# Rearranging three places of a fused two-block network kernel: the zeroing of a scratch array, the rows of maxima in causal attention, and the end of a layer

## The chip, the cores and the metric

The kernel runs on one core of one Trainium2 chip. The metric is the device time of one execution in microseconds (us). Three executions before the change took 4994.17, 4994.56 and 4994.9 us; their median is 4994.56.

## The reference

The input `x` is 4 x 1024 tokens of 128 channels (4096 tokens). Two blocks follow one another, each `x = x + s * silu(g)` with two branches over the same layernorm. Cut to what matters:

```python
xn = layernorm(x)                              # no weights
# block 1
s = attn_in_key_tiles(xn)                      # softmax inside each tile of 128 keys, the 8 tiles averaged by sums
h = xn + causal_attn(rope(conv3(layernorm(xn)) @ attn_w)) @ proj_w   # 16 heads of 8, 1024 tokens
g = h + moe(layernorm(h))                      # top-1 of 4 experts, 512 hidden, silu gate
x = x + s * silu(g)
xn = layernorm(x)
# block 2
s = causal_attn(xn @ w_qkv.T) @ w_proj.T       # 16 heads of 8
g = xn
for i in range(6):                             # 6 layers, 16 heads of 64, windows of 32
    g = g + local_attention(rotary(l2norm(q)), rotary(l2norm(k)), v) @ Wo[i]   # qkv of shift_tokens(g)
    n = layernorm(shift_tokens(g)) * ln_g[i] + ln_b[i]
    a, gate = split(n @ W1[i] + b1[i])         # 341 each
    g = g + (a * gelu(gate)) @ W2[i] + b2[i]
x = x + s * silu(g)
```

The experts work on tokens that are ordered by expert: the kernel scatters them into arrays `sorted_in` in DRAM, whose unused places must be zero.

## The kernel before

The program is one chain of stages, and each stage is one block in which every engine has its own written-out list: TensorE (PE), VectorE (DVE), ScalarE (ACT), GpSimd (POOL) and SyncE (SP, which only issues transfers and waits). A stage opens when the one before it is done on all engines, SP's waits included. Inside a stage the order of each engine is the order of the code, and engines meet by counting semaphores. Activations lie as 128 channels by 4096 tokens; a chunk is 512 tokens (`CH`), a tile 128 (`P`), PSUM is eight banks of 512 f32.

The stages in order: constants, layernorm `ln0`, `tile_attention`, layernorm `ln1`, `causal_convolution`, `causal_inputs`, `causal_attention` `ca0`, `ln2`, `dispatched_experts`, `ln3`, `causal_inputs`, `causal_attention` `ca1`, `shift_tokens`, `layers`, `gate_and_store`.

*The start.* `layernorm` takes a list `fetches`: SP (line 150) issues them all and then waits for all of them (line 152). For `ln0` the list has the remaining constants and tile attention's weights, at most 64 KB each, and last two transfers that fill the two arrays `sorted_in` (19 blocks of 128 x 128 f32, 64 KB, each) from one block of zeros `blank`. In `tile_attention` SP had nothing to do. There POOL first clears the stacks of causal attention (`clear_stacks`, lines 493 to 502) and then scales probabilities (line 465).

*Causal attention.* The work is 16 groups `G` (4 sequences of 1024 tokens by 4 groups of `HG` = 4 heads). A group is 12 units (`UNITS`: 512 queries by 128 keys), and each unit two slots (`two`: a pair of heads); per slot PE makes scores, ACT the exponentials, PE the weighted sums. The scores include minus the row's maximum through two extra rows of the stack `queries`, at `SHIFT_ROW`: the negated maximum in bf16 and its remainder. So while group `G` is worked, the maxima of `G + 1` are made between its slots (`between`, `maximum`, order in `MAXIMA` and `BETWEEN`): PE makes scores once more, in the pair banks 5 and 6 or in the lone bank 7, and DVE reduces them. A bank is taken by `take_pair` or `take_lone` when DVE or ACT has left it. At unit `ROWS_UNIT` = 8 all maxima of the next group are there. DVE negates them into `neg_parts` (`make_rows`), PE turns them into rows (`turn_rows`, line 880): eight products of [128, 8] into the pair banks. ACT copies the rows (`copy_rows`, line 953), SP places them in the next stack by four transfers (`place`, line 753), and the first score of the next group waits for `placed` (line 904). SP also collects the sums of each head and loads the stacks (`load_stack`, line 513). Finished sequences are projected in two halves, `mix`, by a product in the lone bank (line 888) at the units that `FINISH` names; of the 15 changes of group in a stage, 6 have a `mix` at unit 9. `copy_rows` for group `G + 1` stands in ACT's list behind unit 9's first slot.

*Layers.* `steps` lays a tile's operations at fixed distances over 32 tiles (of 128 tokens): `(do, late)` runs `do` for tile `n - late` in step `n`, and `last(...)` only at the last tile. Of a tile, `turn_p` (1653) transposes probabilities, ACT copies them (`out_p`, 1818), `weigh` (1703) makes the heads' outputs, `out_o` (1823) copies them, `project` and `project_rest` (1710) apply `wo`. Behind the last tile begins the second half of the layer, chunk by chunk: `turn` (1730) and `back` (1737) transpose for the layernorm, DVE's `centre` (1974, 1976) and the sums, `square_of` (1846), `norm_invert` (1851, 1853: roots of one of the groups of chunks), `norm_out` (1859), and then the products of the gate (1768) and of the other half (1770), `gelu` (1890), its product on DVE, `down` (1748). `low` (1840) copies what the next shift needs. GELU has its own table in ACT, loaded before the first one (`ACT_TABLE_LOAD`, line 1890).

```python
                    steps((make_next_q, 0), (make_k, 0), (turn_q, 1), (project, 3), (last(lambda: turn(1)), 2), (turn_k, 1),
                          (project_rest, 3), (turn_p, 2), (score, 1), (last(lambda: turn(0)), 1), (make_v, 0), (weigh, 2),
                          (last(lambda: turn(2)), 2))
                    back(0)
```

## Time and profile before

| what | value |
|---|---|
| median of three runs | 4994.56 us |
| profiled execution, its own time | 5013.37 us |
| its span | 5011.6 us |
| PE busy | 4437.7 us (89%) |
| PE weight loads | 2774.2 us (55%) |
| DVE busy | 3689.3 us (74%) |
| ACT busy | 2775.2 us (55%) |
| POOL busy | 2162.7 us (43%) |
| mean granted clock of PE | 0.951 |
| instructions | 169931 |
| DMA queues | 204.72 MB; q1 14.5% of 16 engines, the instruction queues q8 0.8% and q14 0.1% |

The profile is of one execution, which took 5013.37 us, while the three runs without a profile took some 4994.6. Busy times can overlap between engines; PE is the busiest. Of its 40 slices (125 us each) PE is busy by 2 tenths in the first, by 5 to 9 tenths in the next 13, by 9 in all from slice 15 on but the last (8). Weight loads (PEld) run beside products. The granted clock is a share of full speed: 1.00 is 2.4 GHz, 0.50 is 1.2 GHz.

### The profile page before, as it was taken

The page shows a single profiled execution, that of the slowest core. Times are in us where ns is not written, and L with a number is a line of the kernel's source. Part 1 is how long each engine was busy: PE and PEld are TensorE (multiplying, and loading weights), DVE is VectorE, ACT ScalarE, POOL GpSimd, SP SyncE. Part 2 cuts the span into 40 slices and gives each one's busy share as a digit, 9 for nine tenths or more (in the row PEclk, how much of TensorE's full clock was granted, in tenths as well). Part 3 has the DMA queues.
Part 4 walks back from the last instruction along what each step waited for, and adds up shares of the span by engine and source line. Part 5 has one row for each costly group of instructions (what it writes and reads, how often), then busy time and mean ns, then how long its engine had stood idle before and what let it go on. Part 6 is the DMA issues. An engine that isn't in the chain of part 4 may idle for free. (4 is left out here: it accounts for less than half of the span.)

```text
span 5011.6 us, 169931 instructions
## 1 busy us (share of the span) xinstructions
PE 4437.7 (89%) x75610; PEld 2774.2 (55%) x75610; DVE 3689.3 (74%) x4181; ACT 2775.2 (55%) x3767; POOL 2162.7 (43%) x1739
## 2 busy tenths in 40 slices
PE   2876888595898699999999999999999999999998
PEld 1652333363333267765777476756776577646774
DVE  1667887124788488877888688858987799768885
ACT  1644777233677555655665565655655566545664
POOL 1332000313000066645665466636664566546661
PEclk6997999696999899999999999999999999999999
DMA  1002111112011111111111111111111111111110
GB/s 42 1 25 66 39 45 33 60 36 84 25 43 41 54 40 41 41 49 31 41 41 37 44 41 41 41 44 39 41 39 49 36 41 41 38 42 41 39 40 25
DMA packets 108209, 204.72 MB, mean 41 GB/s; under 512 B 28594, under 2 KB 56882, under 8 KB 105650
## 3 DMA queue, kind: packets, MB, share of 16 engines
q1 hardware_dynamic: 105432, 189.65, 14.5%
q8 instruction: 598, 9.80, 0.8%
q0 software_dynamic: 2048, 4.20, 0.3%
q14 instruction: 131, 1.07, 0.1%
HBM read 67.52 MB, written 22.81 MB: 18 GB/s over the span
## 5 line engine op out<-in xcount | busy, mean ns | idle before, releaser
L2044 POOL TENSOR_TENSOR part_of_layer<-part_of_layer,sine_of_layer 128x512 f32<-128x512 f32 x768 | 963.2, 1276 | 620.7 <-DVE sine_of_layer L1920 620.7
L2055 POOL TENSOR_TENSOR part_of_layer<-part_of_layer,inverse_of_layer 128x1024 f32<-128x1024 f32 x384 | 730.1, 1901 | 261.2 <-ACT inverse_of_layer L1803 246.1
L976 ACT ACTIVATE prob_of_ca<-ps 128x1024 f32<-128x1024 f32 (+3 forms) x768 | 591.9, 814 | 245.4 <-PE ps L850 173.0
L1917 DVE TENSOR_TENSOR part_of_layer<-ps,rope 128x1024 f32<-128x1024 f32 x384 | 466.1, 1214 | 33.0 <-ACT square_of_layer L1791 31.4
L1920 DVE TENSOR_TENSOR sine_of_layer<-ps,rope 128x1024 f32<-128x1024 f32 x384 | 464.8, 1210 | 0.0
L1834 ACT ACTIVATE values_of_layer<-ps 128x1024 f32<-128x1024 f32 x192 | 196.5, 1023 | 458.4 <-PE ps L1684 458.4
L868 PE MATMUL ps<-keys_of_ca,queries_of_ca 64*128 64x512 bf16 (+3 forms) x1536 | 325.8, 341 | 133.9 <-DVE top_of_ca L1008 59.7
L1703 PEld LDWEIGHTS ps<-prob_t_of_layer,mixed_of_layer 64*64 64x64 f32 x12288 | 342.4, 135 | 164.1 <-issue 154.5
L1710 PE MATMUL ps<-heads_out_of_layer,wo 128*128 128x128 f32 x3072 | 417.8, 281 | 13.1 <-ACT heads_out_of_layer L1823 12.1
L1956 DVE TENSOR_REDUCE total_of_layer<-prob_of_layer 128x16 f32<-128x1024 f32 x192 | 234.1, 1219 | 237.9 <-ACT prob_of_layer L1827 237.9
L1610 PE MATMUL ps<-qkv,shifted 128*128 128x512 f32 x768 | 383.2, 621 | 24.0 <-POOL values_of_layer L2058 19.9
L1703 PE MATMUL ps<-prob_t_of_layer,mixed_of_layer 64*64 64x32 f32 x12288 | 392.7, 221 | 13.0 <-ACT prob_t_of_layer L1818 6.7
L1703 PE MATMUL ps<-prob_t_of_layer,values_of_layer 64*64 64x32 f32 x12288 | 391.0, 220 | 12.9 <-issue 12.0
L1710 PEld LDWEIGHTS ps<-heads_out_of_layer,wo 128*128 128x128 f32 x3072 | 383.4, 197 | 16.9 <-ACT heads_out_of_layer L1823 16.9
L1684 PE MATMUL ps<-qkv,shifted 128*64 128x512 f32 x1536 | 383.7, 612 | 7.1 <-issue 7.1
L1008 DVE TENSOR_REDUCE top_of_ca<-ps 128x2 f32<-128x1024 f32 (+1 forms) x320 | 357.3, 1117 | 40.2 <-PE ps L868 24.8
L1623 PE MATMUL ps<-qkv,shifted 128*128 128x512 f32 x768 | 362.8, 595 | 12.0 <-DVE sine_of_layer L1920 12.0
L1703 PEld LDWEIGHTS ps<-prob_t_of_layer,values_of_layer 64*64 64x64 f32 x12288 | 345.2, 135 | 18.8 <-issue 17.4
L1813 ACT ACTIVATE keys_of_layer<-ps 128x1024 f32<-128x1024 f32 x192 | 196.8, 1025 | 248.9 <-PE ps L1642 248.9
L919 PE MATMUL ps<-prob_of_ca,values_of_ca 128*32 128x512 f32 (+3 forms) x3072 | 327.2, 498 | 0.7 <-ACT summed_of_ca L962 0.7
L1964 DVE TENSOR_TENSOR prob_of_layer<-prob_of_layer,total_of_layer 128x1024 f32<-128x1024 f32 x192 | 318.4, 1658 | 6.6
L1671 PE MATMUL ps<-keys_of_layer,queries_of_layer 64*32 64x64 f32 x24576 | 298.7, 228 | 4.1 <-issue 3.2
(237 smaller groups left out, 8831.1 us busy)
## 6 DMA issues: line engine op xcount, KB each, us to landing
mixed_of_layer<-values_of_layer SPq DMA_DIRECT2D x636, 128.0 KB
mixed_of_layer<-values_of_layer SPq DMA_DIRECT2D x264, 64.0 KB
queries_of_ca<-q_parts SPq DMA_DIRECT2D x384, 32.0 KB
keys_of_ca<-k_parts SPq DMA_DIRECT2D x384, 32.0 KB
qkv<-in_qkv SPq DMA_DIRECT2D x6, 1536.0 KB, 6.3
q_parts<-parts_of_ci SPq DMA_DIRECT2D x16, 384.0 KB, 2.5
k_parts<-parts_of_ci SPq DMA_DIRECT2D x16, 384.0 KB
rope<-in_rope SPq DMA_DIRECT2D x6, 1024.0 KB, 8.9
```

The lines of the kernel that those rows point to most:

```text
L919: last = nc.tensor.matmul(ps[h * QUAD:(h + 1) * QUAD, SUM_BANK, j:], values[:, G % 2, kt, h, :], prob[:, i % 2, h, j:], start=kt == 0, sto ...
L976: nc.scalar.activation(prob[:, i % 2, 2 * two:2 * two + 2, j:], ps[:, 2 * two:2 * two + 2, j:], ACT.Exp, scale=scale).then_inc(raised, 1)
L1008: nc.vector.reduce_max(to, pair[:, :, 0:width], AX_X).then_inc(pair_used, 1)
L1610: last = nc.tensor.matmul(two_banks(SCORE_SLOT)[:, a, :], xs[:, tokens(t)], w["qkv"][:, 0, chunk(a)], start=True, stop=True)
L1623: last = nc.tensor.matmul(two_banks(KEY_SLOT)[:, a, :], xs[:, tokens(t)], w["qkv"][:, 1, chunk(a)], start=True, stop=True)
L1684: last = nc.tensor.matmul(two_banks(VALUE_SLOT)[h * DH:(h + 1) * DH, a, :], xs[:, t * P + a * DH:t * P + (a + 1) * DH], w["qkv"][:, 2, chu ...
L1703: last = nc.tensor.matmul(out, src[rows, t % RING * 2 + i // 2, p + e, :], prob_t[rows, p + e, i * WIN:(i + 1) * WIN], start=True, stop=True)
L1710: last = nc.tensor.matmul(two_banks(OUT_SLOT)[:, 0, 0:P], w["o"][:, p, :], heads_out[:, p, :], start=p == 0, stop=p == PAIRS - 1)
L1917: nc.vector.tensor_tensor(part[:, t % 2, side], by_head(slot), table(2 * side, t), ALU.mult).then_inc(parts, 1)
L1920: nc.vector.tensor_tensor(sine[:, side], by_head(slot), table(2 * side + 1, t), ALU.mult).then_inc(parts, 1)
L2044: nc.gpsimd.tensor_tensor(out, out, sine[:, side, :, (1 - to) * half:(2 - to) * half], ALU.add).then_inc(rotated, 1)
L2055: nc.gpsimd.tensor_tensor(part[:, t % 2, side], part[:, t % 2, side], by, ALU.mult).then_inc(scaled, 1)
```

## The change

First, `ln0` no longer has the two zeroing transfers among its fetches. They are handed to `tile_attention` as `blanks`; a new SP block there issues them and waits for both with an own semaphore `blanked`, so that the stage ends not before they have landed.

Second, in causal attention the parts of the maxima lie as [128, part, parity of head, pair of heads, tile], 64 columns, and one product turns all of them into [64, 128] in the lone bank. ACT copies these 64 x 128, and SP places them by two transfers of 2 x 16 pieces of 128 bf16 (256 bytes) in place of four of 2 x 1024. DVE makes the parts by four instructions with the third maxima (one for the negated value, two for the remainder) in place of three. The two `mix` move from unit 9 to unit 10.

Third, in `layers` the last tile's `turn_p` moves ahead of `project_rest`, `turn(1)` behind it, and `back(0)` ahead of the last `project`; on ACT `square_of(1)` is alone behind `out_p`, `norm_invert(0)` comes after `out_o`, and `norm_out(0)` right behind the last tile's `out_o`; the table of GELU is loaded ahead of the last `low`; on DVE `spread_of(0)` and `norm_even(0)` come ahead of `centre(1)`.

```diff
 tile_attention:
+            @block.sync
+            def _(sp):
+                for to, of in blanks:
+                    sp.dma_start(to, of).then_inc(blanked, 16)
+                sp.wait_ge(blanked, 16 * len(blanks))
...
-FINISH = {(0, 9): ("invert", 0), (1, 9): ("mix", 0), (2, 9): ("mix", 1)}
+FINISH = {(0, 9): ("invert", 0), (1, 10): ("mix", 0), (2, 10): ("mix", 1)}
+PLACES = 16 * 2
...
-        top, neg_parts = st.sb("top", [P, TOPS, HG]), st.sb("neg_parts", [P, TILES, HG, 2], BF16)
-        rows = st.sb("rows", [2 * HG, L], BF16)
+        top, neg_parts = st.sb("top", [P, TOPS, HG]), st.sb("neg_parts", [P, 2, 2, HG // 2, TILES], BF16)
+        rows = st.sb("rows", [2 * HG * TILES, P], BF16)
...
                 def place(G):
                     sp.wait_ge(rows_out, G + 1)
-                    for h in range(HG):
-                        row = ROW_HALF * (h % 2) + SHIFT_ROW
-                        sp.dma_start(stacks[G % RING_CA][0][row:row + 2, h // 2, :], rows[2 * h:2 * h + 2, :])\
-                            .then_inc(placed[G % RING_CA], 16)
+                    for e in range(2):
+                        row = ROW_HALF * e + SHIFT_ROW
+                        to = stacks[G % RING_CA][0][row:row + 2, :, :].rearrange("s j (q n) -> s (j q) n", n=P)
+                        sp.dma_start(to, rows[e * HG * TILES:(e + 1) * HG * TILES, :]).then_inc(placed[G % RING_CA], 16)
...
                 def turn_rows(G):
-                    take_pair()
-                    pe.wait_ge(negated, 3 * (G + 1))
-                    for qt in range(TILES):
-                        last = nc.tensor.matmul(pair[0:2 * HG, qt // 4, qt % 4 * P:(qt % 4 + 1) * P],
-                                                neg_parts[:, qt].rearrange("p h s -> p (h s)"), k["ident_b"][:, :],
-                                                start=True, stop=True)
-                    last.then_inc(pair_ready, 1)
+                    take_lone()
+                    pe.wait_ge(negated, 4 * (G + 1))
+                    nc.tensor.matmul(lone[0:2 * HG * TILES, 0:P], neg_parts[:].rearrange("p e s j t -> p (e s j t)"),
+                                     k["ident_b"][:, :], start=True, stop=True).then_inc(lone_ready, 1)
...
                 def copy_rows(G, n):
-                    act.wait_ge(pair_ready, n + 1)
+                    act.wait_ge(lone_ready, n + 1)
...
-                    nc.scalar.activation(rows[:, :], pair[0:2 * HG, :, :].rearrange("p a n -> p (a n)"),
-                                         ACT.Copy).then_inc(pair_used, 1)
+                    nc.scalar.activation(rows[:, :], lone[0:2 * HG * TILES, 0:P], ACT.Copy).then_inc(lone_used, 1)
...
                 for l in range(LAYERS):
-                    steps((make_next_q, 0), (make_k, 0), (turn_q, 1), (project, 3), (last(lambda: turn(1)), 2), (turn_k, 1),
-                          (project_rest, 3), (turn_p, 2), (score, 1), (last(lambda: turn(0)), 1), (make_v, 0), (weigh, 2),
-                          (last(lambda: turn(2)), 2))
-                    back(0)
+                    steps((make_next_q, 0), (make_k, 0), (turn_q, 1), (project, 3), (turn_k, 1), (turn_last_p, 2),
+                          (project_rest, 3), (turn_other_p, 2), (last(lambda: turn(1)), 2), (score, 1), (last(lambda: turn(0)), 1), (make_v, 0), (weigh, 2),
+                          (last(lambda: turn(2)), 2), (last(lambda: back(0)), 2))
...
-                    steps((square_next_q, 0), (square_k, 0), (out_q, 1), (out_k, 1), (out_p, 2), (last(first_invert), 2), (invert, 0),
-                          (out_v, 0), (raise_p, 1), (last(lambda: square_of(0)), 1), (out_o, 2), (shift_low, 4))
+                    steps((square_next_q, 0), (square_k, 0), (out_q, 1), (out_k, 1), (out_p, 2), (last(lambda: square_of(1)), 2), (invert, 0),
+                          (out_v, 0), (raise_p, 1), (last(lambda: square_of(0)), 1), (out_o, 2), (last(lambda: norm_invert(0)), 1), (shift_low, 4))
+                    reach(act, l, fetched, 16 * FETCHES)
+                    norm_out(0)
                     square_of(2)
                     norm_invert(1)
+                    nc.scalar.preload_act_table_set(GELU)
                     reach(act, l, added, NT)
                     low(NCH - 1, False)
-                    reach(act, l, fetched, 16 * FETCHES)
-                    norm_out(0)
```

How the order of instructions moves at three places; the line numbers of the changed kernel are its own.

PE in causal attention, at a change of group that has a `mix`. The names are the operands; `neg_parts` are the negated maxima, `evened` the half sequence that `mix` projects. Before:

```order
L904 MATMUL ps<-queries_of_ca,keys_of_ca 128x384 x2
L850 MATMUL ps<-sb_after_k,sb_ident 128x64 x2
L850 MATMUL ps<-sb_after_k,sb_ident 128x128 x2
L880 MATMUL ps<-sb_ident_b,neg_parts_of_ca 8x128 x8
L888 MATMUL ps<-evened_of_ca,sb_cproj 128x512
L868 MATMUL ps<-keys_of_ca,queries_of_ca 128x256 x2
L850 MATMUL ps<-sb_after_q,sb_ident 128x128 x2
L850 MATMUL ps<-sb_after_q,sb_ident 128x64 x2
L868 MATMUL ps<-keys_of_ca,queries_of_ca 128x256 x2
```

and now:

```order
L909 MATMUL ps<-queries_of_ca,keys_of_ca 128x384 x2
L858 MATMUL ps<-sb_after_k,sb_ident 128x64 x2
L858 MATMUL ps<-sb_after_k,sb_ident 128x128 x2
L887 MATMUL ps<-sb_ident_b,neg_parts_of_ca 64x128
L876 MATMUL ps<-keys_of_ca,queries_of_ca 128x256 x2
L858 MATMUL ps<-sb_after_q,sb_ident 128x128 x2
L858 MATMUL ps<-sb_after_q,sb_ident 128x64 x2
...
L858 MATMUL ps<-sb_after_k,sb_ident 128x64 x2
L858 MATMUL ps<-sb_after_k,sb_ident 128x128 x2
L893 MATMUL ps<-evened_of_ca,sb_cproj 128x512
L876 MATMUL ps<-keys_of_ca,queries_of_ca 128x384 x2
```

Eight products became one, the pair maximum follows it, and the product with `sb_cproj` (`mix`) comes two slots later, before the second maximum of unit 10's first slot.

PE at the end of a layer, from the last full `project` to the first product of the gate (`sine_of_layer` by `w`). A product by `wo` in f32 counts twice in the trace, which has x12 for the six here. Before:

```order
L1710 MATMUL ps<-heads_out_of_layer,wo 128x128 x6
L1730 MATMUL ps<-sb_ident,shifted 128x128 x4
L1710 MATMUL ps<-heads_out_of_layer,wo 128x128 x2
L1653 MATMUL ps<-sb_ident,prob_of_layer 128x128 x8
L1703 MATMUL ps<-prob_t_of_layer,mixed_of_layer 64x32 x4
...
L1703 MATMUL ps<-prob_t_of_layer,values_of_layer 64x32 x4
L1730 MATMUL ps<-sb_ident,shifted 128x128 x4
L1710 MATMUL ps<-heads_out_of_layer,wo 128x128 x8
L1737 MATMUL ps<-sb_ident,part_of_layer 128x128 x4
L1768 MATMUL ps<-sine_of_layer,w 128x512
```

and now:

```order
L1718 MATMUL ps<-heads_out_of_layer,wo 128x128 x6
L1661 MATMUL ps<-sb_ident,prob_of_layer 128x128 x8
L1718 MATMUL ps<-heads_out_of_layer,wo 128x128 x2
L1738 MATMUL ps<-sb_ident,shifted 128x128 x4
L1711 MATMUL ps<-prob_t_of_layer,mixed_of_layer 64x32 x4
...
L1711 MATMUL ps<-prob_t_of_layer,values_of_layer 64x32 x4
L1738 MATMUL ps<-sb_ident,shifted 128x128 x4
L1745 MATMUL ps<-sb_ident,part_of_layer 128x128 x4
L1718 MATMUL ps<-heads_out_of_layer,wo 128x128 x8
L1783 MATMUL ps<-sine_of_layer,w 128x512
```

The transposes of the last tile's probabilities (`prob_of_layer`) follow the first six products of `project` and no longer `project_rest` and `turn(1)`, and `back(0)` (`part_of_layer`) stands ahead of the last `project`.

ACT at the end of a layer. Before:

```order
L1851 ACTIVATE norm_root_of_layer<-norm_total_of_layer 128x4
L1853 ACTIVATE norm_root_of_layer<-norm_root_of_layer 128x4
L1823 ACTIVATE heads_out_of_layer<-ps 128x1024
L1846 ACTIVATE sine_of_layer<-part_of_layer 128x512
L1851 ACTIVATE norm_root_of_layer<-norm_total_of_layer 128x8
L1853 ACTIVATE norm_root_of_layer<-norm_root_of_layer 128x8
L1840 ACTIVATE shifted<-cur 64x512
L1859 ACTIVATE sine_of_layer<-ps,small 128x512
L1890 ACT_TABLE_LOAD
L1890 ACTIVATE square_of_layer<-ps,b 128x512 x2
```

and now:

```order
L1868 ACTIVATE norm_root_of_layer<-norm_root_of_layer 128x4
L1833 ACTIVATE prob_t_of_layer<-ps 128x1024
L1861 ACTIVATE sine_of_layer<-part_of_layer 128x512
L1838 ACTIVATE heads_out_of_layer<-ps 128x1024
L1874 ACTIVATE sine_of_layer<-ps,small 128x512
L1861 ACTIVATE sine_of_layer<-part_of_layer 128x512
L1866 ACTIVATE norm_root_of_layer<-norm_total_of_layer 128x8
L1868 ACTIVATE norm_root_of_layer<-norm_root_of_layer 128x8
L1894 ACT_TABLE_LOAD
L1855 ACTIVATE shifted<-cur 64x512
L1902 ACTIVATE square_of_layer<-ps,b 128x512 x2
```

`norm_out(0)` (from `ps,small`) stands right behind the last copy of `heads_out`, ahead of the second group's square and roots, and the table load stands ahead of `low` (`shifted<-cur`).

## Rows read from the trace of the kernel before

**Rows 1.** Windows: window and length; busy us, count per engine; PE clock, DMA share, GB/s.
```profile
34.00:113.00 79.00, 0.00 (x0) 0.00 (x0) 0.00 (x0) 0.00 (x0) 0.00 (x0) 0.51 0.06 27
```

**Rows 2.** Timeline, start: start, us, engine, line, work, count, [idle before, releaser].
```profile
16.79 1.41 SPq L150 DMA_DIRECT2D sorted_in<-in_blank  x2
...
22.97 6.92 POOL L142 TENSOR_TENSOR centred_of_ln<-centred_of_ln,root_of_ln 128x512 f32<-128x512 f32 x6 [22.54 <-DVE root_of_ln L237]
...
32.63 0.60 ACT L208 ACTIVATE cur<-ps 128x512 f32<-128x512 f32 x1 [0.23 <-PE ps L179]
113.10 0.94 POOL L496 MEMSET zeros_of_ca<- 2x1024 bf16 x1 [83.21 <-POOLq L71]
...
126.64 2.17 ACT L383 ACTIVATE prob_of_ta<-ps,shift_of_ta 128x128 f32<-128x128 f32 x8
...
136.45 3.75 POOL L465 TENSOR_TENSOR prob_of_ta<-prob_of_ta,ratio_of_ta 128x1024 f32<-128x1024 f32 x2
```

**Rows 3.** Timeline, end of tile attention and second layernorm.
```profile
315.14 0.69 ACT L371 ACTIVATE s<-ps,sb_ta_bo 128x512 f32<-128x512 f32 x1 [4.57 <-PE ps L313]
...
316.74 7.22 PEld L167 LDWEIGHTS ps<-sb_centre,cur 128*128 128x128 f32 x64 [2.47 <-issue]
...
326.77 6.92 POOL L142 TENSOR_TENSOR centred_of_ln<-centred_of_ln,root_of_ln 128x512 f32<-128x512 f32 x6 [18.41 <-DVE root_of_ln L237]
```

**Rows 4.** Timeline of PE at a change of group without mix.
```profile
555.49 0.61 PE L880 MATMUL ps<-sb_ident_b,neg_parts_of_ca 128*8 128x128 bf16 x8
557.36 0.28 PE L868 MATMUL ps<-keys_of_ca,queries_of_ca 64*128 64x256 bf16 x2 [1.26 <-ACT rows_of_ca L953]
...
558.01 0.38 PE L868 MATMUL ps<-keys_of_ca,queries_of_ca 64*128 64x512 bf16 x1
...
564.07 0.34 PE L904 MATMUL ps<-queries_of_ca,keys_of_ca 64*128 64x384 bf16 x2
```

**Rows 5.** Timeline of ACT there.
```profile
556.31 1.00 ACT L953 ACTIVATE rows_of_ca<-ps 8x1024 bf16<-8x1024 f32 x1
```

**Rows 6.** Timeline of SP's issues, two changes of group.
```profile
613.84 2.47 SPq L753 DMA_DIRECT2D queries_of_ca<-rows_of_ca  x4
...
641.75 2.47 SPq L753 DMA_DIRECT2D queries_of_ca<-rows_of_ca  x4
```

**Rows 7.** List of DMA issues: count, KB each, median us to landing.
```profile
b<-in_b SPq DMA_DIRECT2D x6, 3.0 KB, 2.6
```

**Rows 8.** Timeline of PE: start of the stage, and a change with mix.
```profile
442.50 1.02 PE L880 MATMUL ps<-sb_ident_b,neg_parts_of_ca 128*8 128x128 bf16 x8 [0.86 <-DVE top_of_ca L1010]
...
444.62 0.39 PE L868 MATMUL ps<-keys_of_ca,queries_of_ca 64*128 64x256 bf16 x2 [0.57 <-ACT rows_of_ca L953]
...
612.50 1.13 PE L888 MATMUL ps<-evened_of_ca,sb_cproj 128*128 128x512 f32 x2
```

**Rows 9.** Timeline of PE: end of the first layer, and of the second.
```profile
2206.95 2.93 PE L1710 MATMUL ps<-heads_out_of_layer,wo 128*128 128x128 f32 x12 [1.63 <-ACT heads_out_of_layer L1823]
2209.67 0.84 PE L1730 MATMUL ps<-sb_ident,shifted 128*128 128x128 f32 x4
...
2210.79 1.04 PE L1653 MATMUL ps<-sb_ident,prob_of_layer 128*128 128x128 f32 x8
...
2220.45 1.10 PE L1768 MATMUL ps<-sine_of_layer,w 128*128 128x512 f32 x2 [1.81 <-ACT sine_of_layer L1859]
...
2225.25 0.60 PE L1730 MATMUL ps<-sb_ident,shifted 128*128 128x128 f32 x4
...
2751.21 1.85 PE L1653 MATMUL ps<-sb_ident,prob_of_layer 128*128 128x128 f32 x8
```

**Rows 10.** Timeline of DVE and ACT, end of the first layer.
```profile
2215.63 0.69 DVE L1974 TENSOR_REDUCE sums_of_layer<-ps 128x4 f32<-128x512 f32 x1 [2.69 <-PE ps L1730]
...
2218.91 0.21 ACT L1853 ACTIVATE norm_root_of_layer<-norm_root_of_layer 128x8 f32<-128x8 f32 x1
...
2220.32 1.28 ACT L1890 ACT_TABLE_LOAD   x1
```

More of the change, by code:

```diff
@@ L53 @@
 LOG_AND_EXP = "natural_log_exp_and_others"
+GELU = "gelu_and_others"
 FIRST_SEM = 150
@@ L267, in tile_task, with tile_attention @@
     return (b, "mix", 0) if at == TILES - 1 else (b - 1, "mix", 1) if b else None
-def tile_attention(nc, ps, k, w, xn, out, stacks, zeros):
+def tile_attention(nc, ps, k, w, xn, out, stacks, zeros, blanks):
     scale = float(1.0 / np.sqrt(C))
@@ L798, in _ @@
                 for slot in range(RING_CA):
-                    sp.wait_ge(placed[slot], 16 * HG * len(range(slot, ALL, RING_CA)))
+                    sp.wait_ge(placed[slot], PLACES * len(range(slot, ALL, RING_CA)))
             @block.gpsimd
@@ L963, in sum_out @@
                                          ACT.Copy).then_inc(acc_out, 1)
-                in_pair = [pieces > 1 for _, pieces in MAXIMA]
-                pairs = sum(in_pair) + in_pair[0]
-                copy_rows(0, pairs)
-                pairs += 1 + sum(in_pair[1:AHEAD])
+                alone = [pieces == 1 for _, pieces in MAXIMA]
+                lones = sum(alone) + alone[0]
+                copy_rows(0, lones)
+                lones += 1 + sum(alone[1:AHEAD])
                 for G in range(ALL):
@@ L978, in _ @@
                             if (i, two) == (ROWS_UNIT + 1, 0) and G + 1 < ALL:
-                                copy_rows(G + 1, pairs)
-                                pairs += 1
+                                copy_rows(G + 1, lones)
+                                lones += 1
+                            lones += (finishing(G, i, two) or ("",))[0] == "mix"
                             for m in maxima_at(G, i, two):
-                                pairs += in_pair[m % NM]
+                                lones += alone[m % NM]
                         if i == 4:
@@ L1020, in make_rows @@
                     negate(nc.vector.tensor_tensor(top[:, half:TILES, :], top[:, half:TILES, :], top[:, TILES:, :], ALU.max))
-                    negate(nc.vector.tensor_scalar(neg_parts[:, :, :, 0], top[:, 0:TILES, :], -1.0, None, ALU.mult))
-                    negate(nc.vector.scalar_tensor_tensor(out=neg_parts[:, :, :, 1], in0=top[:, 0:TILES, :], scalar=-1.0,
-                                                          in1=neg_parts[:, :, :, 0], op0=ALU.mult, op1=ALU.subtract))
+                    tops = top[:, 0:TILES, :].rearrange("p t (j e) -> p t j e", e=2)
+                    high, low = (neg_parts[:, :, part].rearrange("p e j t -> p t j e") for part in range(2))
+                    negate(nc.vector.tensor_scalar(high, tops, -1.0, None, ALU.mult))
+                    for e in range(2):
+                        negate(nc.vector.scalar_tensor_tensor(out=low[:, :, :, e], in0=tops[:, :, :, e], scalar=-1.0,
+                                                              in1=high[:, :, :, e], op0=ALU.mult, op1=ALU.subtract))
                 def invert(b):
@@ L1059, in _ @@
                 maximum(NM)
-                next(pairs)
+                next(lones)
                 for m in range(NM + 1, NM + AHEAD):
@@ L2002, in second_centre @@
                 def second_centre():
-                    centre(1)
                     spread_of(0)
                     norm_even(0)
+                    centre(1)
                 def third_centre():
```

29 lines of the change are left out of this document (16 added, 13 removed).

## The prediction

> **What bounds the kernel now.** I read the page's 40 slices first: TensorE (PE) is near full from slice 15 on, and weakest by far in the first. So I looked in windows there, and followed the timeline of each engine at the three places that the change touches.
>
> At the start, no engine works for 79 us [rows 1]. The last instruction of the first layernorm starts at 32.63 and lasts 0.60; tile attention starts at 113.10 [rows 2]. The layernorm's SyncE (SP) waits there for all its fetches, and the last two are the zeroing of `sorted_in`, issued at 16.79. In the idle window one DMA engine of 16 is busy (share 0.06) at 27 GB/s. The zeros are 2 x 19 blocks of 64 KB, 2.49 MB, so at that rate they take 92 us: 16.8 + 92 is 109, and the stage opens at 113. This explains the gap; the other twelve fetches have 64 KB at most.
>
> In causal attention a group of four heads takes 27.9 us (two `place` issues apart [rows 6]) and PE does nearly all of the pacing, with one hole: after the eight products of `turn_rows` (555.49) it stands 1.26 us until ScalarE (ACT) has copied the rows out of the pair banks [rows 4, 5].
>
> At a layer's end PE and ACT work by turns. PE waits 1.63 for a copy of `heads_out`, and 1.81 for `norm_out(0)`, which stands in ACT's order behind the second norm group and the last `low` [rows 9]. VectorE (DVE) waits for PE there, 2.69 before `centre(2)` [rows 10]: what PE gains at the front of this stretch reaches its end.
>
> **Part 1, zeros beside tile attention.** Removed: the wait. With it gone the stage ends at 33.23 [rows 2], and the next opens as after tile attention, where ACT ends at 315.83 and PE starts at 316.74, 0.91 later [rows 3]. That is 34.14 against 113.10: **79.0 us**. PE would also be warmer than in the idle window (granted clock 0.51), but I take nothing for it: POOL clears the stacks from 113.10, and only behind that comes its first weighting, at 136.45 [rows 2]; that length does not hang on PE. Added: two issues and SP's wait in tile attention. The transfer then runs from about 35 to 131, the stage from 34 to 237 (113.10 to 315.83 now), so its cover is 106 us more than it needs; without cover it would cost the 79 again. Bounds 76 to 82.
>
> **Part 2, rows by one product.** In a group without `mix`, PE spends 2.52 us from 555.49 to the lone maximum at 558.01 [rows 4]. Eight products of 0.61 (555.49 to 556.10, where the hole begins) become one, an eighth, 0.08. The pair maximum and the score need 0.65 (557.36 to 558.01) and no longer wait for the copy, since the rows leave by the lone bank. The lone maximum does: ACT can start the copy at 556.31 as now, and 128 columns instead of 1024 cost about 0.27 (eight 128-column exponentials in 2.17 [rows 2]) where the row has 1.00 [rows 5]. That ends at 556.58 and PE goes on at about 556.65: 1.36 saved, I take **1.35**. Bounds: 0.65 if the copy costs its 1.00 for any width, 1.80 if PE need not wait. Behind the hole PE paces DVE, and all shift together. The stack load by SP that DVE's and PE's unit 8 wants starts from unit 0's sums, so it lies outside the hole and stays as tight as it is.
>
> In a group with `mix` there is no hole to remove: the product of `mix` (612.50) fills it [rows 8]. The change moves `mix` to unit 10, where it costs PE its 1.1 us and about 0.1 for the lone bank. So 1.35 - 1.2 leaves **0.15**, bounds -0.3 and 0.7. Of the 15 row changes in a stage, 6 have a `mix`.
>
> VectorE makes the parts in four small instructions instead of three, 0.2 us more. It is idle before its next pair anyway (the pair maximum it waits for starts at 557.36, or 556.1 now), so nothing.
>
> SP issues two transfers instead of four, 1.25 for 2.47. Their landing isn't shown. Nearest rows: the 3 KB load of `b`, also in small pieces, lands in 2.6 [rows 7]; above, that doubled, 5.2; below, nothing. I take 2.5, since 8 KB go out in each of the two. In the loop, copied at 556.6, issued by 557.9 and landed at 560.4, they are wanted at 562.7 (the score at 564.07 [rows 4], 1.36 earlier), so that nothing is lost up to 4.8. The Trainium skill (DMA: Bandwidth & Descriptors, Specifications) says that pieces under 512 bytes are read and written back, below line rate, which speaks against cutting 2 KB rows into 256-byte pieces. By the rule the sum loses nothing unless it comes to 2.3 us in the loop; the trace has no row to test it.
>
> At a stage's start the pair product stands behind the same copy, at 444.62 after products from 442.50 [rows 8]. In the new form it follows the one product, at 442.6, and the later maxima and the first score move with it: 2.0, less the fourth small instruction, **1.9**. Bounds: -0.4 (two transfers that land late by that) and 2.1. Sum: 2 x (9 x 1.35 + 6 x 0.15 + 1.9) = **29.9**.
>
> **Part 3, end of a layer.** First layer, by the new order. `turn_p` of the last tile stands right behind the twelve products of `project` and no longer behind `turn(1)` and `project_rest` (2209.67 to 2210.79 [rows 9]): 1.12 earlier, and those two run while ACT copies. `weigh` then starts 0.96 earlier, since the copy's wait takes 0.16 back. With `turn(2)` and `back(0)` (0.6) in the shadow of the `heads_out` copy, and `norm_out(0)` right behind that copy, the gate's first product could come at 2220.45 - 1.81 - 0.96 - 0.6 = 2217.1, 3.3 earlier. But ACT is late next. From `centre(2)` (2215.63) to the second group's root (2218.91 + 0.21) are 3.5 us [rows 10]; new: 2214.65 + 3.5 = 2218.15, table load 1.28, `low` 0.5, so `gelu` 0 at 2219.95 against 2221.6 (2220.32 + 1.28). `turn(4)`, now at 2225.25, must follow `centre(3)`, which DVE does behind the product of `gelu` 0: 2219.95 and four instructions of 0.7 (an activation, the product, the two of `centre(3)`) are 2222.8, and `turn(4)` starts at 2222.95: **2.3** saved. PE keeps the pace after that.
>
> In layers 2, 5 and 6 PE runs slower at this place: `turn_p` takes 1.85 against 1.04 [rows 9]. What I move is then longer: `weigh` gains 1.3, the gate 2.6 and `turn(4)`, an estimate, 2.7. I take 2.7. Sum 3 x 2.3 + 3 x 2.7 = **15.0**; bounds 6 (only the weigh step, 6 x 0.96) and 20 (the gate's whole 3.3).
>
> **Sum.** 79.0 + 29.9 + 15.0 = 123.9. The profiled execution took 5013.37 for a span of 5011.6, so it would take 4889.5. The median of the three runs shown is 18.8 lower, 4994.56; the saved waits are the same there: **4870.7 us**.
>
> **Rivals.**
> 1. *Slower: the rows land late.* Each group's first score waits for `placed`. Below 4.8 us of landing nothing is lost; above it each of 30 changes of group pays the excess. To end 10 us slower than now takes 134 us, 4.5 a group: a landing of 9.3. The nearest row stands at 2.6. Time at 9.3: 5005. Chance 0.01.
> 2. *The zeros hold up the instructions.* Instructions come by DMA too (the page has two queues for them), and one engine is busy for 96 us under a stage with much code. A 64 KB block takes 2.4 us at 27 GB/s; some seven loads, each behind a block, give up to 17: 4888. Against it: the first layernorm ran from 16.8 on beside the zeros, and its six scalings on POOL took 6.92 us, the same as those of the second without them [rows 2, 3]. The Trainium skill (Runtime: NRT & Kernel Launch, Instruction fetch mechanics) has each sequencer fetch the next page by DMA while it runs the current one, and by this it could be late here; the trace disagrees as far as one layernorm tells. Chance 0.08.
> 3. *ACT bounds the layer's start.* If the table load and `low` come after everything, `gelu` 0 gains only 1.0: part 3 gives 6, time 4880. Chance 0.13.
> 4. *The lone bank is a new wait.* If the rows' copy costs its 1.00 and `mix` meets a full lone bank, part 2 gives 2 x (9 x 0.65 - 6 x 0.3 + 1.9) = 12: 4889. Chance 0.12.
> 5. *The change doesn't do what it says:* another fetch holds the stage. Then part 1 is 0, time 4950. Chance 0.01, by the arithmetic of bytes.
>
> **How the numbers follow.** The forecast has 0.65. The clock alone moves the end of a layer (0.8 us for one step of eight products [rows 9]), six of them some 5. The range takes in rivals 2 to 4 and, below, the upper bounds of parts 2 and 3 in part: 4858 to 4889. The measurement tells 0.2% (10 us) from no change. All cases but the first end faster by more than that: faster 0.985, same 0.005, slower 0.01.
>
> **What would show it.** Right: tile attention opens at 34; a steady group without `mix` takes 26.6 us and one with it 27.8; the `rows` copy lasts 0.3; the gate's first product comes with no PE idle, and `gelu` 0 some 3 after it. Wrong: PE idle "issue" in tile attention (rival 2), a wait at the first score of a group for `rows_of_ca` (rival 1), a group still at 27.9 (rival 4).

## Result

The changed kernel takes 4867.07 us, the median of four runs (4860.85 to 4872.69), against 4994.73 us for the kernel before beside it (4994.17 to 5000.35). The ratio is 0.9742, with an interval of 0.9725 to 0.9759: 127.7 us less were measured, 123.9 were forecast (4870.7). Its profiled execution took 4860.85. From the page:

```profile
span 4859.0 us, 169452 instructions
...
PE   7959997767998699999999999999999999999998
...
PEclk9979998887999899999999999999999999999999
```

The first of the 40 slices now has PE busy by 7 tenths instead of 2, at a granted clock of 0.9; over the whole span PE is busy for 91% instead of 89%.

**The start.** The timeline of the changed kernel (start, us, engine, line, work, count, idle before and its releaser):

```profile
31.33 1.09 ACT L209 ACTIVATE cur<-ps 128x512 f32<-128x512 f32 x2 [0.21 <-PE ps L180]
33.30 1.43 SPq L308 DMA_DIRECT2D sorted_in<-in_blank  x2
33.30 0.94 POOL L503 MEMSET zeros_of_ca<- 2x1024 bf16 x1 [3.84 <-POOLq L72]
...
56.65 3.75 POOL L472 TENSOR_TENSOR prob_of_ta<-prob_of_ta,ratio_of_ta 128x1024 f32<-128x1024 f32 x2
...
237.06 1.13 PE L168 MATMUL ps<-sb_centre,cur 128*128 128x128 f32 x8 [1.67 <-PEq L72]
```

These answer to [rows 2, 3] (SPq is SP's issue of a transfer, PEq PE's own sequencer). The layernorm ends at 32.42 (31.33 + 1.09), tile attention opens at 33.30 and not at 113.10, and the zeroing is issued inside it. The stage lasts from 33.30 to 237.06, 203.8 us, as against 203.6 before (113.10 to 316.74). The windows (columns as in [rows 1]) show the zeros still running beside a busy PE, on one engine of 16 (share 0.06) at 25 GB/s, and gone behind 130:

```profile
100.00:130.00 30.00, 28.99 (x170) 20.38 (x168) 20.41 (x51) 19.27 (x56) 9.70 (x6) 1.00 0.06 25
130.00:140.00 10.00, 9.61 (x56) 6.43 (x55) 7.38 (x18) 5.22 (x14) 3.58 (x2) 1.00 0.01 2
```

**A change of group in causal attention.** PE without a `mix`, then ACT:

```profile
471.12 0.24 PE L887 MATMUL ps<-sb_ident_b,neg_parts_of_ca 128*64 128x128 bf16 x1
471.30 0.28 PE L876 MATMUL ps<-keys_of_ca,queries_of_ca 64*128 64x256 bf16 x2
...
472.18 0.39 PE L876 MATMUL ps<-keys_of_ca,queries_of_ca 64*128 64x512 bf16 x1
...
478.25 0.34 PE L909 MATMUL ps<-queries_of_ca,keys_of_ca 64*128 64x384 bf16 x2
```

```profile
471.86 0.26 ACT L958 ACTIVATE rows_of_ca<-ps 64x128 bf16<-64x128 f32 x1
```

Against [rows 4, 5]: one product of 0.24 for eight, the pair maximum 0.18 behind it without a wait, the copy 0.26 long in place of 1.00, and 1.06 us from the rows' product to the lone maximum in place of 2.52. The group takes 26.53 us in place of 27.91. The first score of the next group (478.25) waits for nothing, although the places are issued only at 472.19 and take SP 1.30: the rows of 256-byte pieces landed in 4.8 us or less.

**A change with a `mix`**, the new waits beside it, and the next `mix`:

```profile
522.66 0.23 PE L876 MATMUL ps<-keys_of_ca,queries_of_ca 64*128 64x128 bf16 x2 [0.80 <-DMA queries_of_ca<-zeros_of_ca]
...
527.66 1.12 PE L893 MATMUL ps<-evened_of_ca,sb_cproj 128*128 128x512 f32 x2
...
529.57 0.39 PE L876 MATMUL ps<-keys_of_ca,queries_of_ca 64*128 64x512 bf16 x1 [0.24 <-DVE cur L1044]
...
555.82 1.12 PE L893 MATMUL ps<-evened_of_ca,sb_cproj 128*128 128x512 f32 x2
```

`mix` now stands in the open (527.66), and PE waits once more behind it for VectorE's addition (0.24 at 529.57). At 522.66 PE waits 0.80 for a load of the stack. From this `mix` to the next (555.82) it is 28.16 us. In the kernel before, the next `mix` behind the one of [rows 8] (612.50) is

```profile
640.41 1.12 PE L888 MATMUL ps<-evened_of_ca,sb_cproj 128*128 128x512 f32 x2
```

27.91 later. So a group with `mix` that has no wait for its stack takes 28.17 in place of 27.91: it is 0.26 longer, where a group without `mix` is 1.38 shorter.

**The start of the stage**, against [rows 8] (the second view is the kernel before):

```profile
362.41 0.18 DVE L1025 TENSOR_TENSOR top_of_ca<-top_of_ca 128x16 f32<-128x16 f32 x1
...
364.19 0.61 PE L876 MATMUL ps<-keys_of_ca,queries_of_ca 64*128 64x512 bf16 x2 [0.36 <-ACT rows_of_ca L958]
...
369.19 1.02 PE L909 MATMUL ps<-queries_of_ca,keys_of_ca 64*128 64x512 bf16 x2
```

```profile
440.88 0.17 DVE L1020 TENSOR_TENSOR top_of_ca<-top_of_ca 128x16 f32<-128x16 f32 x1
...
449.19 1.03 PE L904 MATMUL ps<-queries_of_ca,keys_of_ca 64*128 64x512 bf16 x2
```

From VectorE's last of the maxima (362.41) to the first score (369.19) it takes 6.78 us, where it took 8.31 before.

**The end of a layer** (the third), PE and then ACT, against [rows 9, 10]:

```profile
3156.78 1.50 PE L1661 MATMUL ps<-sb_ident,prob_of_layer 128*128 128x128 f32 x8
...
3162.61 2.05 PE L1718 MATMUL ps<-heads_out_of_layer,wo 128*128 128x128 f32 x16
3164.50 1.02 PE L1783 MATMUL ps<-sine_of_layer,w 128*128 128x512 f32 x2
...
3168.99 1.13 PE L1756 MATMUL ps<-square_of_layer,w 128*128 128x512 f32 x2 [0.45 <-DVE square_of_layer L2035]
3170.40 0.63 PE L1738 MATMUL ps<-sb_ident,shifted 128*128 128x128 f32 x4 [0.28 <-DVE part_of_layer L1988]
```

```profile
3162.59 0.78 ACT L1874 ACTIVATE sine_of_layer<-ps,small 128x512 f32<-128x512 f32 x1
...
3165.36 0.21 ACT L1868 ACTIVATE norm_root_of_layer<-norm_root_of_layer 128x8 f32<-128x8 f32 x1
3165.59 1.28 ACT L1894 ACT_TABLE_LOAD   x1
3166.88 0.63 ACT L1855 ACTIVATE shifted<-cur 64x512 f32<-64x512 f32 x1
3167.42 1.24 ACT L1902 ACTIVATE square_of_layer<-ps,b 128x512 f32<-128x512 f32 x2
```

The gate (3164.50) starts with no idle time, where PE stood 1.81 before (in the first layer); GELU 0 comes 2.92 behind it, and `down(0)` (0.45) and `turn(4)` (0.28) now wait for VectorE.

**Stage by stage.** ACT's table loads are marks that stand at the same work in every kernel. Between them, in us, from the one profile of each kernel: A from the first layernorm's roots to those of the second; B both causal attentions, each up to the table load of the stage behind it (`ln2`, `layers`); C the experts' stage; D the six layers; E, part of D, the stretch from ACT's last `raise_p` of a layer (the probabilities' last step, just ahead of `turn_p`) to the second table load behind it, summed over six.

| kernel | A | B | C | D | E |
|---|---|---|---|---|---|
| before | 303.8 | 962.5 | 187.1 | 3250.1 | 220.5 |
| the change | 224.5 | 943.3 | 164.5 | 3225.4 | 202.4 |
| e1 zeros only | 223.3 | 965.3 | 186.2 | 3248.5 | 215.5 |
| e2 rows only | 303.6 | 942.8 | 188.4 | 3250.8 | 217.8 |
| e3 layers only | 304.5 | 964.7 | 186.1 | 3230.6 | 204.3 |
| e4 mix at unit 8 | 224.8 | 939.5 | 188.0 | 3237.5 | 204.2 |
| e5 the change again | 223.4 | 944.2 | 185.3 | 3232.9 | 203.9 |
| e6 load first | 224.7 | 939.1 | 185.3 | 3244.1 | 203.3 |
| e7 PE's order only | 227.0 | 943.4 | 184.8 | 3250.0 | 214.8 |
| e8 ACT's and DVE's only | 224.9 | 944.4 | 184.4 | 3260.6 | 224.9 |
| e9 load first, mix at 8 | 227.6 | 936.7 | 185.6 | 3229.0 | 202.6 |
| e10 and low late | 224.7 | 935.9 | 182.9 | 3234.1 | 201.7 |
| e11 wide zeros | 223.4 | 964.5 | 183.1 | 3245.3 | 219.8 |
| e12 mix at unit 9 | 224.4 | 950.2 | 184.4 | 3230.7 | 205.0 |

The two profiled executions are 152.5 us apart, 25 more than the medians. Column C names most of the difference: the experts' stage, which the change does not touch, took 164.5 us in this one profile and 182.9 to 188.4 in the others. In the kernel before, ACT stands still there while POOL issues its indirect gathers:

```profile
1077.42 0.60 ACT L1325 ACTIVATE gate_of_moe<-ps 128x512 f32<-128x512 f32 x1 [7.38 <-remote]
...
1081.62 0.60 ACT L1296 ACTIVATE block_t_of_moe<-ps 128x512 f32<-128x512 f32 x1 [3.60 <-DMA queries_of_ca<-zeros_of_ca]
...
1086.51 0.60 ACT L1303 ACTIVATE gated_t_of_moe<-ps 128x512 f32<-128x512 f32 x1 [4.29 <-DMA folded_of_ca<-totals]
...
1087.25 1.08 PE L1227 MATMUL ps<-sb_ident,gated_of_moe 128*128 128x128 f32 x4 [11.79 <-ACT gated_t_of_moe L1303]
```

PE loses 11.79 us there, and 5 at another place of the stage; in the profile of the change neither wait is there, in e5, the same kernel in another comparison, both are (11.20 and 4.99). So these 22.6 belong to the chip or the run and not to the change.

### The profile page after: what moved, and what is told of

The parts are those of the page before. It is cut to its first block and busy times, and to the rows that moved or that the text cites. A ratio compares the mean times of both kernels' runs of the same rounds, so it can differ in the third digit from the quotient of the medians.

```text
span 4859.0 us, 169452 instructions
## 1 busy us (share of the span) xinstructions
PE 4413.6 (91%) x75386; PEld 2749.0 (57%) x75386; DVE 3699.8 (76%) x4213; ACT 2755.6 (57%) x3767; POOL 2167.2 (45%) x1739
## 5 line engine op out<-in xcount | busy, mean ns | idle before, releaser
L1711 PEld LDWEIGHTS ps<-prob_t_of_layer,values_of_layer 64*64 64x64 f32 x12288 | 343.1, 135 | 17.6 <-issue 16.2
```

Source lines behind the costliest of these rows:

```text
L1711: last = nc.tensor.matmul(out, src[rows, t % RING * 2 + i // 2, p + e, :], prob_t[rows, p + e, i * WIN:(i + 1) * WIN], start=True, stop=True)
```

## Experiments

The comparisons ran on three chips, on which the kernel before took 5020.72 (e1 to e4), 5020.65 (e5 to e8) and 5008.26 us (e9 to e12). Ratios are to the runs on the same chip, with a 95% interval of 0.13 to 0.17% either way, which is some 7 to 8 us.

**e1: the zeros alone.** The hunks of `tile_attention` and `ln0` on the kernel before.

> The kernel before with part 1 alone. My theory: the wait goes and nothing else moves: 79 to 80.4 us less than before, about 4914 to 4916 (the stretch from the first layernorm to the second shrinks by 80.4, as in the changed kernel's trace); tile attention lasts 202.7 us as before. Rival (the zeros hold up instruction fetch): tile attention lasts up to 17 us longer, 4931. Rival (the 22.6 us that the experts' stage was shorter in the profile of the change come from part 1): 4893.

Measured 4936.46 against 5020.72, ratio 0.9831 (0.9815 to 0.9848). That is 84.3 us less (76 to 93). Column A falls by 80.5, tile attention takes 202.2 us and is not longer, and C stays at 186.2. The first theory stands; both rivals fall.

**e2: the rows alone.** All hunks of `causal_attention`, with `mix` at unit 10.

> The kernel before with part 2 alone. By the two traces a group without mix is 1.37 us shorter, one with mix 0.02 to 0.3 longer, and a stage 9.6 to 11.1 shorter: 4994.7 - 20 = 4975. The prediction's own term was 29.9: 4965. Rival (the groups are late for another reason than part 2): less than 10 saved, 4985 or more.

Measured 4988.91, ratio 0.9935 (0.9919 to 0.9952), 24 to 41 us less. Taken alone the medians speak for 29.9 and against 20. In the traces column B falls by 19.7, the stretches ahead of the two stages by 3.3 together and the one from `ln2` to the experts by 2.7 (see The sum), 25.7 in all, which the interval holds. So the expected 20 was too low, and 29.9 is not what the stages show.

**e3: the layers alone.** The hunks of `layers`.

> The kernel before with part 3 alone. By the ends of the six layers in the two traces 1.0 to 4.4 us each, 18.2 in all: 4976.5. The prediction's term was 15.0: 4979.7. Rival (the clock gives the rest that the layers' stage lost in the profile, 24.7): 4970.

Measured 4996.59, ratio 0.9962 (0.9947 to 0.9977), 12 to 27 less, 24.1 by the medians. Column D falls by 19.5, E by 16.2. The interval holds 15.0 and 18.2 alike.

**e4: `mix` at unit 8.**

```diff
-FINISH = {(0, 9): ("invert", 0), (1, 10): ("mix", 0), (2, 10): ("mix", 1)}
+FINISH = {(0, 9): ("invert", 0), (1, 8): ("mix", 0), (2, 8): ("mix", 1)}
```

> The changed kernel with mix at unit 8 in place of unit 10. Theory A (mix costs at unit 10 its whole product, 1.1 us, and 0.5 of waits behind it, because PE has no hole there; at unit 8 PE waits 1.1 for VectorE and the product fills that): a group with mix takes 27.0 to 27.4 in place of 28.17, 12 groups, 9 to 14 us less than the changed kernel: 4853 to 4858. Rival B (VectorE's addition of 0.69 is what costs, wherever it stands): within 3 us of the changed kernel, 4864 to 4870.

Measured 4891.29, ratio 0.9744 (0.9727 to 0.9760), where e5 has 0.9748. A group with `mix` takes 27.86, not 27.0 to 27.4. PE there:

```profile
519.90 0.39 PE L876 MATMUL ps<-keys_of_ca,queries_of_ca 64*128 64x512 bf16 x2 [1.11 <-DVE top_of_ca L1013]
...
521.63 1.13 PE L893 MATMUL ps<-evened_of_ca,sb_cproj 128*128 128x512 f32 x2
...
523.61 0.39 PE L876 MATMUL ps<-keys_of_ca,queries_of_ca 64*128 64x512 bf16 x1 [0.17 <-DVE cur L1044]
```

The wait of 1.11 stands in unit 7, one slot ahead of the place that I chose, and the product (521.63) still lies in the open. So theory A missed its place. By the medians rival B stands (4891.29, and 4890.89 for e5), but its reason, a constant cost, doesn't quite: the trace has 0.31 a group less, 3.7 in all, too little for the medians to show. `mix` at unit 7 was not tried.

**e5: the change again.**

> The changed kernel once more, beside the others and beside the kernel before on the same chip. The parts alone gave 84.3, 31.8 and 24.1 less by their medians. If they are additive and those medians are right, 140 less than before here; by my sum from traces (80.1 + 19.3 + 14.9 and some 4 in the rest of the layers) 114 to 119; the first comparison had 127.7. The experts' stage, unchanged, took 164.5 us in the changed kernel's profile and 186 to 188 in every other one: if that is a property of chip or run, it takes 187 here; if the change shortened it, 164.5.

Measured 4890.89 against 5020.65, ratio 0.9748 (0.9732 to 0.9764): 129.8 less (118 to 135), as much as at first, on a chip where both are some 25 us longer. The 140 that the medians of the three parts add up to lie outside the interval, the 119 of the traces at its edge. The experts' stage took 185.3.

**e6: the stack load ahead of the collects.**

```diff
-                    collect(G)
                     if G + RING_CA < ALL:
                         sp.wait_ge(scored, 2 * NU * (G + 1))
                         load_stack(sp, loaded[G % RING_CA], stacks, zeros, q_parts, k_parts, G + RING_CA)
+                    collect(G)
```

The wait that it is meant to end is this one in the changed kernel (products for the maxima, us in total, times, longest), below the same wait in the kernel before:

```profile
PE ps L876 <- DMA queries_of_ca<-zeros_of_ca: 5.1, 9, 1.0
```

```profile
PE ps L868 <- DMA queries_of_ca<-zeros_of_ca: 3.3, 8, 0.6
```

> The changed kernel, with SP loading the stack of group G + 2 ahead of the collects of group G, so that the load starts about 5 us earlier in a group. Theory (the groups that take 26.8 to 29.0 instead of 26.53 or 28.17 waited for that load, 11.6 us of PE idle put down to it in 18 places, weight loads and products counted apart): all groups without mix take 26.53 and those with mix 28.17, 4 to 7 us less than e5. Rival (the collects are then late for ACT's copies of the sums): as long as e5 or longer.

The 11.6 of the expectation counts these waits twice, at the weight loads and at the products. Measured 4889.66, ratio 0.9738 (0.9721 to 0.9754). That wait is no longer listed, all groups inside the stages but two take 26.53 or 28.17 (those two 28.53 and 26.30), and column B is 5.1 below e5. The median is only 1.2 below, where 4 to 7 were expected: column D of this profile is 11 above e5, by more than any such gain. The mechanism is shown, the gain in the whole is not.

**e7: of part 3 only PE's order.**

> Parts 1 and 2 and of part 3 only PE's order (turn_p of the last tile ahead of project_rest and turn(1), back(0) ahead of the last project); ACT and DVE in their old order. Theory: from the last raise_p to the second table load of a layer (old 36.4 on average, new 33.9) it gains what turn_p and weigh gain, 1.0 to 1.1 a layer, 6 to 7 in all; the gate's first product still waits for norm_out(0), some 3 us. 8 longer than e5. Rival (PE's order is the whole gain): as e5.

Measured 4910.53, ratio 0.9783 (0.9766 to 0.9799), 19.6 above e5, where 8 were expected. E is 214.8, only 3.6 below the 218.4 of the four kernels with the old end (before, e1, e2, e11) and not 6 to 7. It is 10.9 above e5; the rest of the 19.6 lies in other parts of the layers (column D is 17.1 above e5). End of a layer, ACT and PE:

```profile
3736.86 0.21 ACT L1867 ACTIVATE norm_root_of_layer<-norm_root_of_layer 128x8 f32<-128x8 f32 x1
...
3738.27 0.76 ACT L1873 ACTIVATE sine_of_layer<-ps,small 128x512 f32<-128x512 f32 x1
...
3739.17 1.10 PE L1782 MATMUL ps<-sine_of_layer,w 128*128 128x512 f32 x2 [1.80 <-ACT sine_of_layer L1873]
```

The gate waits 1.80 for `norm_out(0)`, which stands behind the second group's root as before. `turn_p` is earlier and the wait takes most of that over.

**e8: of part 3 only ACT's and DVE's order.**

> Parts 1 and 2 and of part 3 only ACT's and DVE's order; PE in its old order. Theory: turn_p and weigh stay as before; back(0) comes on PE only after the last project, so that ACT's norm_out(0) waits for it and the second norm group behind it is later by about 2: GELU 0 comes no earlier, 0 to 1 us a layer lost: 15 to 21 longer than e5. Rival (norm_out(0) was the bound, so this part alone gives 1.4 a layer): 6 longer than e5.

Measured 4914.12, ratio 0.9787 (0.9770 to 0.9803), 23.2 above e5; E is 224.9, 6.5 above the old end and 21.0 above e5.

```profile
3203.93 0.60 PE L1745 MATMUL ps<-sb_ident,part_of_layer 128*128 128x128 f32 x4
...
3204.63 0.78 ACT L1867 ACTIVATE sine_of_layer<-ps,small 128x512 f32<-128x512 f32 x1 [2.64 <-PE ps L1745]
...
3205.55 1.10 PE L1776 MATMUL ps<-sine_of_layer,w 128*128 128x512 f32 x2 [1.02 <-ACT sine_of_layer L1867]
...
3210.75 1.12 PE L1756 MATMUL ps<-square_of_layer,w 128*128 128x512 f32 x2 [1.09 <-DVE square_of_layer L2028]
```

`norm_out(0)` waits for `back(0)` (3203.93), which PE does only behind the last `project`, and ACT's square for the second group stands behind it. GELU 0 is later, and `down(0)` waits 1.09. The theory holds. The two halves alone are worth -3.6 and +6.5, together -14.7: neither order does it without the other.

**e9: e4 and e6 together.**

> e4 and e6 together: the stack load ahead of the collects, mix at unit 8. If both gains add (27.86 in place of 28.17 for a group with mix; no group waits for its stack): the two stages take 936 us together where the changed kernel has 943 to 944; 7 to 8 us less than the changed kernel, a ratio to before of about 0.973 where e5 had 0.9748. If they are one and the same gain, 939.

Measured 4879.58 against 5008.26, ratio 0.9741 (0.9728 to 0.9754). Column B is 936.7, as expected: the gains add. With e10 this is the shortest version in causal attention, 7 us below the change in B; by its ratio it can't be told from the change (0.9742, 0.9748).

**e10: e9, and `low` behind the first GELU.**

```diff
-                    reach(act, l, added, NT)
-                    low(NCH - 1, False)
                     for u, (c, f) in enumerate(units):
...
+                        if u == 0:
+                            reach(act, l, added, NT)
+                            low(NCH - 1, False)
```

> e9, and in a layer ACT copies the last chunk for the next shift (low, 0.63 us) behind the first GELU and not ahead of it. Theory (ACT bounds the start of the second half of a layer): from the last raise_p to the second table load 0.4 to 0.7 less a layer, 33.3 in place of 33.9, 2.5 to 4 in all. Rival (the table load is what ACT waits out, and PE's 0.45 of idle goes elsewhere): nothing.

Measured 4882.37, ratio 0.9752 (0.9738 to 0.9765). GELU 0 now follows the table load directly. From `weigh` to the second table load each of the six layers takes 25.21 in place of 25.73, so the table load and the copy do bound this stretch, and 0.52 a layer is gained there, 3.1 in all. By the measure of the expectation, from `raise_p` on, four layers took 33.1 to 33.4 but two took 34.3, since the part ahead of `weigh` varies; E is only 0.9 less, and the median is 2.8 above e9. So the mechanism is shown and the gain in the whole is not.

**e11: the zeros in another form, at their old place.**

```diff
-                          [(to.rearrange("(b p) c -> b p c", p=P), a["blank"].unsqueeze(0).to_broadcast([BLOCKS, P, P]))
+                          [(to.rearrange("(b p) c -> p b c", p=P), a["blank"].unsqueeze(1).to_broadcast([P, BLOCKS, P]))
```

> The kernel before, unchanged but for the form of the two zeroing transfers, which stay in the first layernorm's fetches: the same 2.49 MB, laid out as 128 rows by 19 blocks of 512 bytes each instead of 19 blocks of 64 KB. Theory (the 79 us are the time of one DMA engine of 16, which the outermost count of 19 got; with 128 outermost all 16 work): the zeros take 92 / 16 = 6 us and some more for small pieces, the wait is gone without moving it, ratio to before 0.983 to 0.985 as e1. Rival (the pieces or the writes to DRAM bound it, not the engine): a good part of the 79 us stays, ratio 0.99 or more.

Measured 4930.91 against 5008.26, ratio 0.9851 (0.9836 to 0.9866). The timeline and the windows of the start:

```profile
16.63 3.50 SPq L150 DMA_DIRECT2D sorted_in<-in_blank  x2
...
34.59 0.94 POOL L496 MEMSET zeros_of_ca<- 2x1024 bf16 x1 [4.25 <-SPq L302]
```

```profile
20.00:26.00 6.00, 2.89 (x20) 2.41 (x19) 5.38 (x12) 4.08 (x8) 2.59 (x3) 0.84 1.10 315
26.00:32.00 6.00, 5.34 (x23) 4.25 (x23) 2.40 (x3) 3.24 (x6) 4.33 (x4) 0.50 0.06 19
```

All 16 engines work (share 1.10 for 6 us, 315 GB/s), and just behind 26 the zeros are through. Tile attention opens at 34.59 with the transfers still in the layernorm's list, and column A is 223.4 as in e1. The 79 us came from a transfer on one engine, and its form alone takes them away. The form changes two things at once, the outermost count and the size of the pieces (64 KB, now 512 bytes); no run separates them. The Trainium skill (DMA: Bandwidth & Descriptors, Why a DMA increments its semaphore by 16 and not by 1) spreads a transfer over the largest number of engines, up to 16, that divides the size of the slowest dimension on both of its sides. By it the count alone decides. The trace agrees: 19 got one, 128 got sixteen.

**e12: `mix` at unit 9.**

> The changed kernel with mix back at unit 9, behind turn_rows. In the old form mix filled the hole in which PE waited for the copy of the rows, and a group with mix took 28.15 to 28.3. Theory: the hole is now 0.32, so the product of 1.06 costs 0.8 to 1.6 there: 27.4 to 28.2, and the whole is within 5 us of e5. Rival (mix holds the lone bank against the rows, so unit 10 was needed): 28.5 or more, 5 us or more above e5.

Measured 4892.49, ratio 0.9769 (0.9755 to 0.9784). A group with `mix` takes 28.46:

```profile
525.03 1.13 PE L893 MATMUL ps<-evened_of_ca,sb_cproj 128*128 128x512 f32 x2 [0.89 <-ACT rows_of_ca L958]
```

`mix` waits 0.89 for the lone bank, from which ACT copies the rows. Column B is 6.0 above e5. Beside e9 on the same chip the median is 12.9 longer, and B 13.5. So the rival holds, if narrowly by its number: the move to unit 10 was needed with the rows in the lone bank, and is worth about 0.3 a group and some waits for the stack. The "28.15 to 28.3" of the expectation is not the old time of a group with `mix`, but of one that waits for its stack too; without that wait it was 27.91.

## Why the prediction was right, point by point

**Part 1, forecast 79.0 (76 to 82).** Column A is 304.0 on average in the three kernels with the wait and 224.9 in the ten with the zeros beside tile attention: 79.0. The cover held as reckoned; the zeros ended before 130, the stage at 237. Rival 2 (instruction fetch) is excluded for tile attention by the stage's length, 203.8 against 203.6. In the experts' stage engines do stand still beside other transfers, see below.

**Part 2, forecast 29.9.** Column B falls by 20.6 (964.2 on average in the four old ones, 943.6 in the change, e2, e5, e7 and e8), and the stretches ahead of the two stages by 1.3 and 2.0: about 24. The step for a group without `mix` was right, 1.38 for 1.35. Three steps failed, all to the same side:
- "leaves 0.15" for a group with `mix`: it loses 0.26 (28.17 for 27.91). The product at unit 10 costs 1.64 over a plain group and not 1.2; VectorE's addition behind it makes PE wait once more (0.24). Over 12 groups this step is 4.9 of the 6 us that part 2 has too much. The forecast took `mix` to have filled the hole, which is right; what it had wrong is the price of the new place.
- "The stack load by SP ... stays as tight as it is": it doesn't quite. PE's products wait 5.1 us for it in place of 3.3. The load starts behind the collects, which SP issues in 4.5 us of its own time, and a group that is 1.4 shorter meets it sooner. Moving the load (e6) takes away the old part of this wait together with the new.
- "1.9" at a stage's start: 8.31 against 6.78 is 1.5. The later maxima are paced by VectorE and take back a part.

With these steps as measured the sum would be 22.9: 18 x 1.38, less 12 x 0.26 and 1.8, and 2 x 1.5. What was priced at nothing was right otherwise: SP's two transfers land in time, and the fourth small instruction of VectorE costs no time in the loop.

**Part 3, forecast 15.0.** Column E is 218.4 on average in the four with the old end and 203.7 in the seven with the new one (the change, e3 to e6, e9, e12): 14.7, and column D falls by 15.8. The traces bear out its two halves: from the last `raise_p` to `weigh` a layer takes 8.22 on average in place of 9.23, 1.0 less, and from `weigh` to the second table load 25.73 in place of 27.17 (27.0 in some layers, 27.6 in others), 1.4 less. What bounded it was right too, ACT's chain to GELU 0 and then `centre(3)`. One step was right in size and wrong in its reason: I gave layers 2, 5 and 6 a slower clock as a property of theirs. `turn_p` takes 1.04 in some layers and 1.91 in others, in other layers in each profile: 1.91 in the first and fourth of the change, in the first, second and sixth of e5, the same kernel, but 1.04 to 1.23 in the first five of e1 and 1.87 in its sixth. The granted clock at `turn_p` goes with it. Windows of the first layer and of the sixth in the change (columns as in [rows 1]):

```profile
2082.50:2084.40 1.90, 1.90 (x11) 1.90 (x10) 0.00 (x0) 0.00 (x0) 1.00 (x1) 0.50 0.00 0
4765.50:4766.50 1.00, 1.00 (x12) 1.00 (x11) 0.55 (x2) 0.35 (x2) 0.00 (x0) 1.00 0.05 16
```

At 0.50 the eight products take 1.91, at 1.00 they take 1.04. In which layer the clock is low differs between executions, so the right form of the term was one average of about 2.5 a layer. Rival 3 (ACT bounds the start, 1.0 a layer) did not come: ACT's chain moved with `centre(2)` as the sum had it.

**The other rivals.** Rival 1 (the rows land late) did not come, since the first score waits for nothing. Rival 5 did not: the stage opens at 33.30. Of rival 4 the first condition is false (the copy takes 0.26). Its second, a `mix` that meets a full lone bank, is real only at unit 9 (0.89 in e12); at unit 10 the loss of 0.26 a group is as large as the 0.3 that it named, for another reason.

**The sum.** 79.0 + 24 + 15.8 is 119; the two comparisons of whole runs gave 127.7 and 129.8, with an interval of some 8 either way. In nine of the ten kernels with part 2 the stretch from the roots of `ln2` to the experts is 2 to 4 us shorter (61.6 on average for 64.3; e12 has 63.1), without an edit there; in the change the granted clock ahead of the router's work is 0.65 to 0.67, where it was 0.55 to 0.60 before (both levels, 0.50 and 1.00, occur in such a window). That is the only further piece that I found. The total was closer than its parts, and that is luck: 6 too much in part 2 stood against the 9 to 11 that the traces don't give to any part.

## What to carry to other kernels

Where a stage ends with all engines idle and one queue busy, read how many DMA engines the transfer has before moving it: another order of its dimensions gave the same 79 us as hiding it did. Orders on engines that hand work to each other are one edit: half of such a change can cost time where the whole gains, so it is priced along the chain of both. And when a loop gets shorter, look at what is issued at a fixed pace beside it; the waits for it grow. A product that fills a hole is free only there: when the hole goes, price its new place with the waits that follow it.

## What the runs showed that I had not expected

- ACT and VectorE stand still in the experts' stage, for 5 to 6.5 and for 8 to 13 us of PE's time, while POOL issues indirect gathers, in thirteen of fourteen profiles. The profile names no plausible releaser (a transfer of an earlier stage, "remote"). That instructions arrive late beside the gathers was not tested and stays open, and so does why one execution was free of it; it makes 20 us of 5000, more than part 3. In the comparison of the change the kernel before took some 20 us less than in its own profile (4994.7, 5013.4), so both kernels may have been free of it there; no profile of that kernel shows it.
- The comparisons differ by more than a small gain: the kernel before took 4994.7, 5020.7, 5020.7 and 5008.3 (medians) in the four of them, the last three on different chips. Gains of 3 to 5 us (e4, e6, e10) were visible in a stage of the trace and in no median.
